# Output projection of a local-attention layer as three rounded products instead of one full float32 product

## Chip, cores and metric

One core of one Trainium2 chip. The metric is device time in microseconds (us) of one execution. "Rounded" stands for the type float32r of the program (printed as fp32r where it is written), "full float32" for plain f32.

## The reference

A sandwich of three blocks on x, 4 sequences of 512 tokens by 128 channels: x + 0.5 F(norm x), then a one-head attention whose softmax runs over an axis of length one, so that it is a sum of values, then x + 0.5 F(norm x) again. F has 6 layers of local attention and feed-forward. What the change touches is the last line of this:

```python
def attn_layer(x, Wqkv, qs, ksc, Wo):          # x: (4, 512, 128), 16 heads of 64
    q, k, v = split_heads(x @ Wqkv)
    q, k = l2norm(q) * qs, l2norm(k) * ksc      # then rotary embedding with scales
    out = local_attention(q, k, v)              # window 32, each looks one window back
    return merge_heads(out) @ Wo                # (4, 512, 1024) @ (1024, 128)
```

## The kernel before, in words

The work is cut in **units**: a unit is 128 tokens by 8 of the 16 heads (half h = U % 2). 8 units (UPS) make one sequence, 32 (UPL) one layer, 192 (UPP) one pass over the 6 layers; two passes make 384 units. All engines run the same loop over **slots** n (L1013 on TensorE, L607 ScalarE, L781 VectorE, L463 GpSimd, L356 the DMA queue of SyncE), and in a slot each takes its steps in an order written out by hand. Engines are kept in step by counting semaphores alone.

TensorE in slot n (L1014 to L1040): queries and keys of unit n+2 from Wqkv (project_qk), transposes of unit n (query_heads, key_heads), the mask, values of unit n (project_v), scores(n), in one slot of eight down (feed-forward), then transposes of the probabilities of unit n-1 (prob_major, L923), the output projection of unit n-2 (project_out, L951), and the weighing of values of unit n-1 (weigh_values, L934). In slots n%8 = 3, 4, 6 and 0 a step of the feed-forward follows; gated (n%8 = 0) is the long one.

project_out multiplies for each of 4 head pairs a 128x128 block of Wo (stationary) by ot (128x128, moving) and adds up in the PSUM tile tr0: 4 products in full float32. In the trace each is two LDWEIGHTS and two MATMUL of 128x128. The other projections are done with rounded numbers already: x and W are each split in a rounded high part and a rounded low part, and hi·hi + hi·lo + lo·hi is added up (project, L850; gated, L983). Each of these products is one LDWEIGHTS and one MATMUL.

ScalarE copies PSUM to SBUF: outputs(n-2) makes ot from o_ps (L573), weights_out(n-1) makes pt (L567), squares (L527), queries (L543), first_guess (L534, L537). VectorE: prob_sums(n-1) (L734, L737), rotate(n+2) (L699, L705), add_output(n-2) (L745), row_maxima and differences of n (L719, L726), square_sums(n+2) (L712). GpSimd: scale_probs(n-1) (L425), inverse_norms and normalise of n+1 (L433 to L448), then weight splitting where due, add_rotated(n+2) (L419).

Weights: Wqkv of the next layer comes in 6 blocks of 128x512 through a ring of two staging buffers: with m the slot in the layer, block m//4 is loaded at m%4 = 0 (load_block, L286), its high part is made by ScalarE at m%4 = 2 (split_high, L509), its low part by GpSimd at m%4 = 3 (split_low, L398). So splits fall in slots m = 3, 7, 11, 15, 19, 23. Wo comes in one DMA of 512 KB at m = 5 (load_wo, L296) to a double-buffered tile. At m = 11 GpSimd also splits W1 (L403), and at 13, 17, 21, 25 it makes rotary tables (L410).

Of the kernel before, what the change touches and what calls it, by code (L numbers as in the profile page):

```python
# [37 lines left out]
ONE, DMA_ONE = 1, 16  # L38
BLOCKS = 6
HS = SEQ // 2  # L40
# [35 lines left out]
def build(nc, x, w_qkv, w_o, Wqkv, Wo, W1, W2, scales_dram, vecs_dram, rot_dram, mask_dram, ident_dram, out):  # L76
    ctx = ExitStack()
    with ctx:
# [3 lines left out]
        def sem(name):  # L82
            return ctx.enter_context(nc.semaphore(name))
# [11 lines left out]
        staging = [sb(f"staging{i}", [P, HALF]) for i in range(2)]  # L95
        wqkv_hi = [sb(f"wqkv_hi{i}", [P, 3 * INNER], F32R) for i in range(2)]
        wqkv_lo = [sb(f"wqkv_lo{i}", [P, 3 * INNER], F32R) for i in range(2)]
        wo = [sb(f"wo{i}", [P, 2, PAIRS, P]) for i in range(2)]
        w1 = sb("w1", [P, 2 * HID])
# [35 lines left out]
        rden = [sb(f"rden{h}", [P, PAIRS * 2]) for h in range(2)]  # L135
        pt = [sb(f"pt{h}", [P, PAIRS, P]) for h in range(2)]
        ot = [sb(f"ot{h}", [P, 2, PAIRS, KEYS]) for h in range(2)]

# [141 lines left out]
        def _(sp):  # L280
# [5 lines left out]
            def load_block(g, b):  # L286

                k = g * BLOCKS + b
                if k >= 2:
                    sp.wait_ge(wqkv_split, k - 1)  # L290
                sp.dma_start(staging[k % 2][:, :], Wqkv[g % DEPTH, :, b * HALF:(b + 1) * HALF]).then_inc(block_in[k % 2], 16)

            def load_wo(g):

                sp.wait_ge(y_ready, ONE + UPL * max(0, g - 1))
                sp.dma_start(wo[g % 2][:, :, :, :].rearrange("p h a n -> p (h a n)"), Wo[g % DEPTH, :, :]).then_inc(wo_in, 16)  # L296

# [51 lines left out]
            for b in range(2, BLOCKS):  # L349
                load_block(0, b)  # L350
            load_wo(0)
            load_w1(0)
            load_w2(0)
            for p in range(PASSES):
                stage_tokens(p, p * SEQS * DEPTH)
                for n in slots(p):  # L356
                    if live(p, n):
                        shift_values(n)
                    if (it := staged_for(p, n, 0)) is not None:
                        stage_tokens(p, it)  # L360
                    if (it := ffn_of(p, n, MEAN_AT - 1)) is not None:
                        shift_ffn(it)
                    g, m = layer_slot(p, n)
                    if g + 1 < PASSES * DEPTH:
                        if m >= 0 and m % 4 == 0 and m // 4 < BLOCKS:
                            load_block(g + 1, m // 4)
                        if m == 5:
                            load_wo(g + 1)
                        if m == 13:
                            load_w1(g + 1)  # L370
                    if m == 12 and g > 0:
                        load_w2(g)
# [6 lines left out]
        def _(pool):  # L379
# [76 lines left out]
            for t in range(TPS):  # L456
                rotary_tables(0, t)
            for b in range(BLOCKS):
                split_low(0, b)
            for p in range(PASSES):  # L460
                for s in range(SEQS):
                    macaron_std(2 * p * SEQS + s)
                for n in slots(p):  # L463
                    if live(p, n - 1):
# [22 lines left out]
        def _(act):  # L487
# [16 lines left out]
            def split_high(g, b):  # L504

                k = g * BLOCKS + b
                act.wait_ge(block_in[k % 2], 16 * (k // 2 + 1))
                act.wait_ge(v_ready, ONE + UPL * max(0, g - 1))
                nc.scalar.activation(wqkv_hi[g % 2][:, b * HALF:(b + 1) * HALF], staging[k % 2][:, :], ACT.Copy  # L509
                                     ).then_inc(wqkv_hi_ready, 1)  # L510
# [53 lines left out]
            def weights_out(U):  # L564
                act.wait_ge(ptp_ready, ONE + U + 1)
                act.wait_ge(o_ready, ONE + max(0, U - 1))
                nc.scalar.activation(pt[U % 2][:, :, :].rearrange("p a n -> p (a n)"), tr1[:, :], ACT.Copy).then_inc(pt_ready, 1)  # L567

            def outputs(U):

                act.wait_ge(o_ready, ONE + U + 1)
                act.wait_ge(y_ready, ONE + max(0, U - 1))
                nc.scalar.activation(ot[U % 2][:, :, :, :].rearrange("p g a q -> p g (a q)"), o_ps[:, :, 0:PAIRS * KEYS],  # L573
                                     ACT.Copy).then_inc(ot_ready, 1)
# [22 lines left out]

            for b in range(BLOCKS):
                split_high(0, b)
            act.wait_ge(vecs_in, 32)  # L600
            nc.scalar.preload_act_table_set("natural_log_exp_and_others")
            for p in range(PASSES):
                for s in range(SEQS):
                    macaron_squares(2 * p * SEQS + s)
                act.wait_ge(zeros_ready, 8)
                tokens_high(p * SEQS * DEPTH)
                for n in slots(p):  # L607
                    after_gated = ffn_of(p, n - 1, GATED_AT) is not None
# [48 lines left out]
        def _(dve):  # L657
            for released in (summed, ss_ready, rot_parts, max_ready, dif_ready, rden_ready, y_added, xs_split,
                             fvar_ready, fn_ready, fn_split, hid_ready, xa_ready):
                dve.sem_inc(released, ONE)  # L660
# [69 lines left out]
            def prob_sums(U):  # L730
# [45 lines left out]
            for p in range(PASSES):  # L776
# [44 lines left out]
        def _(pe):  # L821
# [39 lines left out]
            def project_qk(U):  # L861
# [3 lines left out]
                if U % UPL == 0:  # L865
                    pe.wait_ge(wqkv_split, BLOCKS * (U // UPL + 1))
                project(qk_ps[:, 0, :], U, 0)
# [66 lines left out]
            def weigh_values(U):  # L934
# [3 lines left out]
                pe.wait_ge(vhead_in[h], TG * 16 + 16)  # L938
                pe.wait_ge(ot_ready, ONE + U)
                for a in range(PAIRS):  # L940
                    for ws in range(2):
                        for hp in range(2):
                            for gg in range(2):
# [3 lines left out]
                                    o_ps[hp * DH:(hp + 1) * DH, gg, at:at + WIN], (vn if ws else vs)[h][rows, 2 * a + hp, :],  # L947
                                    pt[h][rows, a, c * WIN:(c + 1) * WIN], start=True, stop=True, skip_group_check=True)
                last.then_inc(o_ready, 1)

            def project_out(p, U):  # L951
                h, g = U % 2, U // UPL
                pe.wait_ge(ot_ready, ONE + U + 1)
                if live(p, U + 2):
# [149 lines left out]
```

## Time and profile before

| | |
|---|---|
| time, median of 3 runs | 3490.75 us (3485.07 to 3491.98) |
| the profiled execution | 3489.94 us |
| its span, first to last instruction | 3488.1 us |
| mean granted TensorE clock | 0.983 |
| busy share PE, PEld, DVE, ACT, POOL | 95%, 77%, 75%, 63%, 75% |

PE is TensorE's matmul, PEld its weight load, which lies beside matmuls; DVE is VectorE, ACT ScalarE, POOL GpSimd, SP SyncE. A MATMUL record has the time until its last result, so neighbouring records overlap: what one costs in a row of them is the distance from start to start, and the busy share of PE says little. The chain of waits is followed back from the last instruction, each time to what released it; its times don't overlap.

### The profile page before, as it was taken

To read this page: it belongs to the slowest core of one execution; us is meant where nothing else is said; L and a number is where in the kernel's file an instruction comes from. 1 tells how busy PE (TensorE), PEld (TensorE's weight loads), DVE (VectorE), ACT (ScalarE), POOL (GpSimd) and SP (SyncE) were. 2 spreads that over 40 slices of the span, in tenths; PEclk is the share of its full clock that TensorE was granted. 3 is DMA by queue.
4 is the path that set the end of the run, shared out by engine and by line. 5 is a ranking of instruction groups with operands and counts; after the bars stand their busy time and mean duration, and the time that the engine had idled before them with its cause. 6 is when DMAs were issued, how large, how long until landed. Compare 5 with 4: busy or idle time off the path is not lost.

```text
span 3488.1 us, 149929 instructions
## 1 busy us (share of the span) xinstructions
PE 3326.3 (95%) x63806; PEld 2681.4 (77%) x63806; DVE 2632.2 (75%) x4403; ACT 2200.0 (63%) x4154; POOL 2606.3 (75%) x2894
## 2 busy tenths in 40 slices
PE   6999999999999999999789999999999999999997
PEld 4777778777777777877667777777777778778875
DVE  3777777877787877777458787778787778777773
ACT  3666666666666666666436666666666666666664
POOL 5877787787787777787348778877877877777772
PEclk8999999999999999999879999999999999999998
DMA  2222221221221222221112222212212212221111
GB/s 81 70 55 52 64 56 52 64 61 48 63 62 49 61 62 53 62 63 45 30 26 72 55 54 65 57 51 63 61 47 64 62 51 66 55 56 47 52 46 35
DMA packets 117856, 195.41 MB, mean 56 GB/s; under 512 B 23756, under 2 KB 36552, under 8 KB 117192
## 3 DMA queue, kind: packets, MB, share of 16 engines
q1 hardware_dynamic: 117192, 185.82, 19.6%
q8 instruction: 507, 8.31, 1.0%
q14 instruction: 157, 1.29, 0.1%
HBM read 33.71 MB, written 1.05 MB: 10 GB/s over the span
## 4 chain that ended last, share of the span: by engine, by line
PE 72%; POOL 16%; ACT 6%; issue 3%; DVE 1%; POOLq 0%; DMA 0%; ACTq 0%; SPq 0%; DVEq 0%
PE o_ps L946 10%; PE tr L961 8%; PE s_ps L917 7%; PE tr L930 5%; PE qk_ps L857 5%; POOL rotated L419 5%; PE qk_ps L859 4%; POOL rotated L448 4%; PE qk_ps L858 4%; PE f_ps L1007 4%; PE tr L884 4%; PE tr L857 3%; PE tr L897 3%; POOL prob L425 3%; ACT sq L527 2%
## 5 line engine op out<-in xcount | busy, mean ns | idle before, releaser
L419 POOL TENSOR_TENSOR rotated<-rotated 128x1024 f32<-128x1024 f32 x384 | 917.7, 2390 | 23.7 <-DVE rotated L705 23.7
L448 POOL TENSOR_TENSOR rotated<-rotated,rn 128x1024 f32<-128x1024 f32 x384 | 731.0, 1904 | 30.1
L425 POOL TENSOR_TENSOR prob<-prob,rden 128x512 f32<-128x512 f32 x384 | 436.6, 1137 | 417.2 <-DVE rden L737 413.4
L699 DVE TENSOR_TENSOR rotated<-qk_ps,rot 128x1024 f32<-128x1024 f32 x384 | 469.8, 1223 | 368.0 <-ACT sq L527 362.8
L705 DVE TENSOR_TENSOR rotated<-qk_ps,rot 128x512 f32<-128x512 f32 x768 | 490.4, 679 | 0.0
L917 PEld LDWEIGHTS s_ps<-kt,qt 64*32 64x32 f32 x24576 | 359.5, 107 | 139.6 <-issue 139.6
L712 DVE TENSOR_REDUCE ss_floor<-sq 128x16 f32<-128x1024 f32 x384 | 463.9, 1208 | 0.0
L573 ACT ACTIVATE ot<-o_ps 128x512 f32<-128x512 f32 x384 | 230.6, 601 | 317.4 <-PE o_ps L946 317.4
L917 PE MATMUL s_ps<-kt,qt 64*32 64x64 f32 x24576 | 421.5, 218 | 0.0
L543 ACT ACTIVATE qt<-tr 128x512 f32<-128x512 f32 x384 | 230.1, 599 | 294.5 <-PE tr L884 291.5
L961 PE MATMUL tr<-ot,wo 128*128 128x128 f32 x3072 | 414.6, 278 | 0.0
L527 ACT ACTIVATE sq<-qk_ps 128x1024 f32<-128x1024 f32 x384 | 397.5, 1035 | 17.6 <-PE qk_ps L859 17.6
L567 ACT ACTIVATE pt<-tr 128x512 f32<-128x512 f32 x384 | 229.7, 598 | 281.8 <-PE tr L930 281.7
L946 PE MATMUL o_ps<-pt,vs 64*64 64x32 f32 x12288 | 392.3, 222 | 1.4 <-ACT pt L567 1.4
L946 PE MATMUL o_ps<-pt,vn 64*64 64x32 f32 x12288 | 384.3, 219 | 0.0
L961 PEld LDWEIGHTS tr<-ot,wo 128*128 128x128 f32 x3072 | 374.1, 192 | 2.1 <-issue 1.2
L857 PE MATMUL qk_ps<-wqkv_hi,xs_hi 128*128 128x512 f32 x768 | 352.7, 459 | 21.2 <-DVE rotated L705 18.0
L946 PEld LDWEIGHTS o_ps<-pt,vs 64*64 64x64 f32 x12288 | 326.5, 134 | 48.1 <-ACT pt L567 1.9
L734 DVE TENSOR_REDUCE den<-prob 128x8 f32<-128x512 f32 x384 | 260.5, 678 | 126.0 <-ACT prob L553 125.7
L946 PEld LDWEIGHTS o_ps<-pt,vn 64*64 64x64 f32 x12288 | 328.7, 135 | 0.0
L859 PE MATMUL qk_ps<-wqkv_hi,xs_lo 128*128 128x512 f32 x768 | 306.5, 399 | 0.0
L858 PE MATMUL qk_ps<-wqkv_lo,xs_hi 128*128 128x512 f32 x768 | 305.0, 397 | 0.0
(151 smaller groups left out, 6960.5 us busy)
## 6 DMA issues: line engine op xcount, KB each, us to landing
vs<-vn SPq DMA_DIRECT2D x384, 192.0 KB
vs<-vtail SPq DMA_DIRECT2D x384, 64.0 KB, 2.5
vtail<-vn SPq DMA_DIRECT2D x384, 64.0 KB, 2.2
staging<-layer_wqkv_dram SPq DMA_DIRECT2D x72, 256.0 KB, 3.7
wo<-layer_wo_dram SPq DMA_DIRECT2D x12, 512.0 KB, 4.6
xs<-xa SPq DMA_DIRECT2D x48, 128.0 KB, 2.3
fs<-xa SPq DMA_DIRECT2D x48, 128.0 KB, 2.6
xs<-xa SPq DMA_DIRECT2D x48, 127.8 KB, 3.2
```

What stands on the lines that cost most here:

```text
L419: nc.gpsimd.tensor_tensor(rot_c[h], rot_c[h], rot_s[h], ALU.add).then_inc(rot_added, 1)
L425: nc.gpsimd.tensor_tensor(prob[h][:, :, :], prob[h][:, :, :], rden[h][:, :].unsqueeze(2).to_broadcast([P, 2 * PAIRS, KEYS]), ALU.mult).the ...
L448: nc.gpsimd.tensor_tensor(folded, folded, rn[:, :].unsqueeze(2).to_broadcast([P, 2 * UH, DH]), ALU.mult).then_inc(qkn_ready, 1)
L527: nc.scalar.activation(sq[:, :, :].rearrange("p a d -> p (a d)"), qk_ps[:, :, :].rearrange("p a n -> p (a n)"), ACT.Square, scale=SQUARE_S ...
L699: nc.vector.tensor_tensor(rot_c[h], src, part(0, 0, DH), ALU.mult)
L705: last = nc.vector.tensor_tensor(rot_s[h][:, :, :, to:to + H2], src[:, :, :, lo:lo + H2], part(1, lo, H2), ALU.mult)
L712: nc.vector.tensor_reduce(ss_floor[:, :, 0], sq[:, :, :], AX_X, ALU.add).then_inc(summed, 1)
L857: nc.tensor.matmul(dst, hi, wqkv_hi[g % 2][:, cols], start=True, stop=False)
L859: return nc.tensor.matmul(dst, lo, wqkv_hi[g % 2][:, cols], start=False, stop=True)
L917: last = nc.tensor.matmul(s_ps[c * WIN:(c + 1) * WIN, (2 * a + gg) * KEYS:(2 * a + gg + 1) * KEYS], qt[h][rows, a, w * WIN:(w + 1) * WIN], ...
L946: last = nc.tensor.matmul(o_ps[hp * DH:(hp + 1) * DH, gg, at:at + WIN], (vn if ws else vs)[h][rows, 2 * a + hp, :], pt[h][rows, a, c * WIN ...
L961: last = nc.tensor.matmul(tr0[:, 0:P], wo[g % 2][:, h, a, :], ot[h][:, :, a, :], start=a == 0, stop=a == PAIRS - 1)
```

## The change

Wo is no longer a tile of its own. It is loaded as blocks 6 and 7 of the staging ring and split into high and low parts that lie behind those of Wqkv. The attention outputs are split too: ScalarE's copy from o_ps is rounded (ot_hi), and a new VectorE instruction makes ot_lo = o_ps - ot_hi in slot n for unit n-2, after prob_sums(n-1). The o_ps tile is free again after that instruction. pt, ot_hi and ot_lo have one buffer each (pt and ot had two). project_out makes 12 rounded products in place of 4 full ones.

```diff
-BLOCKS = 6
+BLOCKS = 8
+WQKV_BLOCKS = 6
...
-        wo = [sb(f"wo{i}", [P, 2, PAIRS, P]) for i in range(2)]
...
+        pt = sb("pt", [P, PAIRS, P])
+        ot_hi = sb("ot_hi", [P, 2, PAIRS, KEYS], F32R)
+        ot_lo = sb("ot_lo", [P, 2, PAIRS, KEYS], F32R)
...
 load_block(g, b):
+                src = (Wqkv[g % DEPTH, :, b * HALF:(b + 1) * HALF] if b < WQKV_BLOCKS
+                       else Wo[g % DEPTH, :, (b - WQKV_BLOCKS) * HALF:(b - WQKV_BLOCKS + 1) * HALF])
+                sp.dma_start(staging[k % 2][:, :], src).then_inc(block_in[k % 2], 16)
...
-            load_wo(0)
...
-                        if m == 5:
-                            load_wo(g + 1)
...
 GpSimd and ScalarE at the start (split_low / split_high):
-            for b in range(BLOCKS):
+            for b in range(WQKV_BLOCKS):
...
+                if p == 0:          # after macaron_std / after tokens_high
+                    for b in range(WQKV_BLOCKS, BLOCKS):
+                        split_low(0, b)
...
 split_high:
-                act.wait_ge(v_ready, ONE + UPL * max(0, g - 1))
+                act.wait_ge(y_ready, ONE + UPL * max(0, g - 1))
...
 weights_out:
-                act.wait_ge(o_ready, ONE + max(0, U - 1))
+                act.wait_ge(o_ready, ONE + U)
...
 outputs:
-                act.wait_ge(y_ready, ONE + max(0, U - 1))
+                act.wait_ge(y_ready, ONE + U)
...
+            def outputs_low(U):
+                dve.wait_ge(ot_ready, ONE + U + 1)
+                nc.vector.tensor_tensor(ot_lo[:, :, :, :].rearrange("p g a q -> p g (a q)"), o_ps[:, :, 0:PAIRS * KEYS],
+                                        ot_hi[:, :, :, :].rearrange("p g a q -> p g (a q)").bitcast(F32), ALU.subtract
+                                        ).then_inc(ot_split, 1)
...
                     if live(p, n - 1):
                         prob_sums(n - 1)
+                    if live(p, n - 2):
+                        outputs_low(n - 2)
...
 project_qk:
-                    pe.wait_ge(wqkv_split, BLOCKS * (U // UPL + 1))
+                    pe.wait_ge(wqkv_split, BLOCKS * (U // UPL) + WQKV_BLOCKS)
...
 weigh_values:
-                pe.wait_ge(ot_ready, ONE + U)
+                pe.wait_ge(ot_split, ONE + U)
...
 project_out:
-                pe.wait_ge(ot_ready, ONE + U + 1)
+                pe.wait_ge(ot_split, ONE + U + 1)
...
-                    pe.wait_ge(wo_in, 16 * (g + 1))
+                    pe.wait_ge(wqkv_split, BLOCKS * (g + 1))
                 for a in range(PAIRS):
-                    last = nc.tensor.matmul(tr0[:, 0:P], wo[g % 2][:, h, a, :], ot[h][:, :, a, :],
-                                            start=a == 0, stop=a == PAIRS - 1)
+                    at = WQKV_BLOCKS * HALF + (h * PAIRS + a) * P
+                    hi, lo = wqkv_hi[g % 2][:, at:at + P], wqkv_lo[g % 2][:, at:at + P]
+                    nc.tensor.matmul(tr0[:, 0:P], hi, ot_hi[:, :, a, :], start=a == 0, stop=False)
+                    nc.tensor.matmul(tr0[:, 0:P], hi, ot_lo[:, :, a, :], start=False, stop=False)
+                    last = nc.tensor.matmul(tr0[:, 0:P], lo, ot_hi[:, :, a, :], start=False, stop=a == PAIRS - 1)
```

## Rows read from the trace of the kernel before

**Rows 1.** Page: chain of waits, share of the span by engine and line.
```profile
PE 72%; POOL 16%; ACT 6%; issue 3%; DVE 1%; POOLq 0%; DMA 0%; ACTq 0%; SPq 0%; DVEq 0%
PE o_ps L946 10%; PE tr L961 8%; PE s_ps L917 7%; PE tr L930 5%; PE qk_ps L857 5%; POOL rotated L419 5%; PE qk_ps L859 4%; POOL rotated L448 4%; PE qk_ps L858 4%; PE f_ps L1007 4%; PE tr L884 4%; PE tr L857 3%; PE tr L897 3%; POOL prob L425 3%; ACT sq L527 2%
```

**Rows 2.** Chain in order of time, 1513 to 1536 us: start, us, what.
```profile
1513.82 0.44 PE tr L884 x4
...
1516.94 0.58 PE tr L930 x4
1517.52 0.93 PE tr L961 x8
1518.45 1.06 PE o_ps L946 x64
...
1532.30 1.01 POOL prob L425
...
1533.35 0.65 PE tr L930 x4
1534.01 0.89 PE tr L961 x8
```

**Rows 3.** Waits: engine, tile, line, waited for: us in total, times, longest.
```profile
PEld tr L930 <- POOL prob L425: 68.7, 80, 3.9
DVE rotated L699 <- ACT sq L527: 362.8, 267, 4.2
```

**Rows 4.** Groups with shapes apart: busy us, mean ns of one, idle before.
```profile
L961 PEld LDWEIGHTS tr<-ot,wo 128*128 128x128 f32 x3072 | 374.1, 192 | 2.1 <-issue 1.2
L858 PEld LDWEIGHTS qk_ps<-wqkv_lo,xs_hi 128*128 128x128 f32 x768 | 146.2, 190 | 28.7 <-issue 11.0
L903 PEld LDWEIGHTS s_ps<-mask,ident 128*128 128x128 bf16 x384 | 37.6, 98 | 0.0
L973 PE MATMUL f_ps<-mean_mat,fsq 128*128 128x1 f32 x384 | 52.2, 257 | 2.3 <-ACT fd L580 2.3
```

**Rows 5.** Timeline, engine PE: start, us, then as above; L998 to L1000 are rounded.
```profile
1500.27 0.28 PE L998 MATMUL f_ps<-fn_hi,w_hi 128*128 128x256 f32 x1
...
1502.14 0.28 PE L999 MATMUL tr<-fn_lo,w_hi 128*85 128x256 f32 x1
...
1524.65 1.08 PE L961 MATMUL tr<-ot,wo 128*128 128x128 f32 x8
...
1535.89 1.05 PE L973 MATMUL f_ps<-mean_mat,fsq 128*128 128x1 f32 x8
```

**Rows 6.** Groups of DVE, POOL and ACT, columns as in rows 4.
```profile
L674 DVE TENSOR_TENSOR xa<-rotated,tr 128x512 f32<-128x512 f32 x6 | 4.1, 687 | 8.3 <-PE tr L846 8.3
L398 POOL TENSOR_TENSOR wqkv_lo<-staging,wqkv_hi 128x512 fp32r<-128x512 f32 x72 | 92.9, 1292 | 6.5 <-ACT wqkv_hi L509 6.5
L509 ACT ACTIVATE wqkv_hi<-staging 128x512 fp32r<-128x512 f32 x72 | 44.7, 622 | 8.7 <-DMA staging<-layer_wqkv_dram 8.7
```

**Rows 7.** Timeline of DVE, the slots n%8 = 2 and 3.
```profile
1515.47 0.74 DVE L774 SCALAR_TENSOR_TENSOR xa<-f_ps,vecs,xa 128x512 f32<-128x512 f32 x1
1516.33 1.22 DVE L699 TENSOR_TENSOR rotated<-qk_ps,rot 128x1024 f32<-128x1024 f32 x1
...
1522.24 0.20 DVE L737 RECIPROCAL rden<-den 128x8 f32<-128x8 f32 x1
1523.62 1.23 DVE L699 TENSOR_TENSOR rotated<-qk_ps,rot 128x1024 f32<-128x1024 f32 x1 [1.17 <-ACT sq L527]
```

**Rows 8.** Timeline of PE in slot n%8 = 0, with a split, then without.
```profile
1563.93 1.10 PE L917 MATMUL s_ps<-kt,qt 64*32 64x64 f32 x64
1565.74 0.66 PE L930 MATMUL tr<-ident,prob 128*128 128x128 f32 x4 [0.70 <-POOL prob L425]
...
320.34 1.10 PE L917 MATMUL s_ps<-kt,qt 64*32 64x64 f32 x64
321.37 0.66 PE L930 MATMUL tr<-ident,prob 128*128 128x128 f32 x4
```

More of the change, by code:

```diff
@@ L95, in build @@
         staging = [sb(f"staging{i}", [P, HALF]) for i in range(2)]
-        wqkv_hi = [sb(f"wqkv_hi{i}", [P, 3 * INNER], F32R) for i in range(2)]
-        wqkv_lo = [sb(f"wqkv_lo{i}", [P, 3 * INNER], F32R) for i in range(2)]
-        wo = [sb(f"wo{i}", [P, 2, PAIRS, P]) for i in range(2)]
+        wqkv_hi = [sb(f"wqkv_hi{i}", [P, BLOCKS * HALF], F32R) for i in range(2)]
+        wqkv_lo = [sb(f"wqkv_lo{i}", [P, BLOCKS * HALF], F32R) for i in range(2)]
         w1 = sb("w1", [P, 2 * HID])
@@ L135, in build @@
         rden = [sb(f"rden{h}", [P, PAIRS * 2]) for h in range(2)]
-        pt = [sb(f"pt{h}", [P, PAIRS, P]) for h in range(2)]
-        ot = [sb(f"ot{h}", [P, 2, PAIRS, KEYS]) for h in range(2)]
+        pt = sb("pt", [P, PAIRS, P])
+        ot_hi = sb("ot_hi", [P, 2, PAIRS, KEYS], F32R)
+        ot_lo = sb("ot_lo", [P, 2, PAIRS, KEYS], F32R)
         fs = sb("fs", [P, SEQ])
@@ L170, in build @@
         block_in = [sem(f"block_in{i}") for i in range(2)]
-        wo_in = sem("wo_in")
         w1_in = sem("w1_in")
@@ L213, in build @@
         ot_ready = sem("ot_ready")
+        ot_split = sem("ot_split")
         y_ready = sem("y_ready")
@@ L290, in load_block @@
                     sp.wait_ge(wqkv_split, k - 1)
[L291 to L296, printed above, removed]
+                src = (Wqkv[g % DEPTH, :, b * HALF:(b + 1) * HALF] if b < WQKV_BLOCKS
+                       else Wo[g % DEPTH, :, (b - WQKV_BLOCKS) * HALF:(b - WQKV_BLOCKS + 1) * HALF])
+                sp.dma_start(staging[k % 2][:, :], src).then_inc(block_in[k % 2], 16)
             def load_w1(g):
@@ L565, in weights_out @@
                 act.wait_ge(ptp_ready, ONE + U + 1)
-                act.wait_ge(o_ready, ONE + max(0, U - 1))
-                nc.scalar.activation(pt[U % 2][:, :, :].rearrange("p a n -> p (a n)"), tr1[:, :], ACT.Copy).then_inc(pt_ready, 1)
+                act.wait_ge(o_ready, ONE + U)
+                nc.scalar.activation(pt[:, :, :].rearrange("p a n -> p (a n)"), tr1[:, :], ACT.Copy).then_inc(pt_ready, 1)
             def outputs(U):
                 act.wait_ge(o_ready, ONE + U + 1)
-                act.wait_ge(y_ready, ONE + max(0, U - 1))
-                nc.scalar.activation(ot[U % 2][:, :, :, :].rearrange("p g a q -> p g (a q)"), o_ps[:, :, 0:PAIRS * KEYS],
+                act.wait_ge(y_ready, ONE + U)
+                nc.scalar.activation(ot_hi[:, :, :, :].rearrange("p g a q -> p g (a q)"), o_ps[:, :, 0:PAIRS * KEYS],
                                      ACT.Copy).then_inc(ot_ready, 1)
@@ L596, in gates @@
                                          bias=vecs[0:m, l, 3 + NCH + j:4 + NCH + j]).then_inc(gate_ready, 1)
-            for b in range(BLOCKS):
+            for b in range(WQKV_BLOCKS):
                 split_high(0, b)
@@ L606, in _ @@
                 tokens_high(p * SEQS * DEPTH)
+                if p == 0:
+                    for b in range(WQKV_BLOCKS, BLOCKS):
+                        split_high(0, b)
                 for n in slots(p):
@@ L657, in _ @@
         def _(dve):
-            for released in (summed, ss_ready, rot_parts, max_ready, dif_ready, rden_ready, y_added, xs_split,
+            for released in (ot_split, summed, ss_ready, rot_parts, max_ready, dif_ready, rden_ready, y_added, xs_split,
                              fvar_ready, fn_ready, fn_split, hid_ready, xa_ready):
@@ L947, in weigh_values @@
                                     o_ps[hp * DH:(hp + 1) * DH, gg, at:at + WIN], (vn if ws else vs)[h][rows, 2 * a + hp, :],
-                                    pt[h][rows, a, c * WIN:(c + 1) * WIN], start=True, stop=True, skip_group_check=True)
+                                    pt[rows, a, c * WIN:(c + 1) * WIN], start=True, stop=True, skip_group_check=True)
                 last.then_inc(o_ready, 1)
```

## The prediction, made before the changed kernel was run

> **What bounds the kernel now.** I read the chain of waits first, since busy shares mislead on TensorE. TensorE has 72% of the chain and GpSimd 16%; project_out (L961) alone has 8% of 3488 us, 279 us [rows 1]. So the step that the change rewrites lies on the path that sets the end. Next, the chain in order of time, to see how often it does: in slot n%8 = 2 it runs through prob_major, project_out and weigh_values without a gap, and eight L961 instructions hold it for 0.89 to 0.93 us. In the slot after, it leaves TensorE and comes back only by way of GpSimd's scale_probs (L425), at prob_major of the next slot, 1533.35. The project_out that TensorE did meanwhile isn't on the chain [rows 2]. The third view, the waits, counts these detours: TensorE waited 80 times for scale_probs, 68.7 us together, 0.86 us each [rows 3]. 384 - 80 = 304 units have their project_out on the chain; the share says 279 / 0.89 = 313. The two counts agree; I take 310.
>
> **The change part by part.**
>
> *project_out, instructions.* Before: 4 products, each two loads and two matmuls, 8 pairs. After: 3 rounded products for each of 4 pairs of heads, each one load and one matmul, 12 pairs. The question is what a rounded pair costs at 128 moving columns; no row has that. What sets the pace of the present pairs? L961 goes at 0.89 / 8 = 0.111 us a pair with 128 moving columns [rows 2]. L973, full float32 with the same 128x128 load but a single moving column, takes 1.05 us for 8 [rows 5], the last of them 0.257 us long [rows 4], so (1.05 - 0.257) / 7 = 0.113 us a pair. 128 columns or 1: the same pace, so it is the load that sets it. The rounded load is no shorter: 190 ns against 192 ns [rows 4]. Nearest rows for the rounded matmul are those of gated: from 1500.27 to 1502.14 there are 16 steps of 256 moving columns, 0.117 us each [rows 5]; the load fits into that. So a rounded pair at 128 columns should go at the pace of its load: **0.112 us**, between 0.110 (the transposes, four pairs of 128 columns in 0.44 us [rows 2], the quickest of that size) and 0.117 (the rounded row with 256 columns). 12 x 0.112 - 8 x 0.112 = **+0.448 us a unit**, between 12 x 0.110 - 0.896 = 0.42 and 12 x 0.117 - 0.896 = 0.51. The array has less to stream than before (12 x 128 columns once, against 4 products in full float32), but if it wasn't the streaming that set the pace, that buys nothing, and the loads went up by half.
>
> The Trainium skill (TensorE: Matmul & The Clock Gate, section LDWEIGHTS) gives a load the time of its columns at 1.2 GHz, 107 ns for 128, whatever the contraction; by that the sum would be 12 x 0.107 - 0.896 = 0.39 us a unit, an estimate, 120 us for 310 units. The trace agrees within 5 ns.
>
> *What of it reaches the end.* On 310 units in full: 310 x 0.448 = **139 us**. On the other 74 the growth eats TensorE's wait for scale_probs, which at 0.86 us on average is longer than 0.45, so it costs nothing there. If these detours were all shorter than that, it would be 384 units.
>
> *Does something hide the growth?* ScalarE's copy of pt lies beside project_out and is done before it already, since weigh_values, which needs both, follows project_out directly (1518.45 in rows 2); nothing is gained there.
>
> *The low part on DVE.* A new 128x512 tensor_tensor with one operand in PSUM and one in SBUF: 0.69 us as L674 [rows 6], 384 x 0.69 = 265 us of DVE. It stands after prob_sums, where DVE waits for squares in 267 of 384 slots, 362.8 us in all, 1.36 us each [rows 3]; there it is covered. The slot without cover is n%8 = 2: the feed-forward's L774 lies behind prob_sums too, and L699 starts at 1516.33 with no idle before it [rows 7]. There rotate(n+2) comes up to 0.69 us later, and with it add_output, row_maxima, differences and square_sums. The next prob_sums then ends about 0.7 us late (L737 at 1522.24 becomes 1522.9, ends 1523.1), the new low part ends at 1523.8, and L699 starts at 1523.62 plus the 0.45 us by which TensorE and so squares have moved: 1524.07. The delay is gone after one slot. GpSimd's scale_probs of that slot starts 0.7 us late, still before the guess of the norms that it waits for next. I take **0**; the bound is rival 3.
>
> *New waits.* project_out and weigh_values(n-1) wait for ot_split, counted up by outputs_low(n-2). Behind that wait stand the rest of TensorE's slot and all who wait for y and o. But before project_out TensorE has waited in prob_major(n-1) for scale_probs(n-1), which takes 1.01 us on the chain [rows 2] after the same prob_sums that outputs_low follows by 0.69: the low part is there first. In the slot of rows 7 it would be made by 1523.8 at the latest, and project_out starts at 1524.65 [rows 5], with the change later still. outputs_low's own wait for ot_ready is met: ScalarE makes outputs(n-2) ahead of the exponentials that prob_sums waits for. Price 0. One buffer of pt: weights_out(n-1) waits for weigh_values(n-2), which ran a slot before. One buffer of ot_hi: outputs(U) waits for project_out(U-1), which on TensorE stands just before the weigh_values(U) that it waits for anyway. split_high's wait on y_ready is met two slots before. All 0.
>
> *Wo through the ring.* Removed: 12 DMAs of 512 KB at m = 5. Added: 24 loads of 256 KB, at m = 24 and 28, on SyncE's queue in slots where the wait for the earlier split (m = 19, 23) is long met; they stand behind the shifts of values and ahead of nothing due in that slot. Added on ScalarE 24 x 0.622 = 15 us, in slots m = 26 and 30, beside waits; on GpSimd 24 x 1.29 = 31 us [rows 6], at m = 27 and 31, that is n%8 = 3 and 7 of the fourth sequence, the only one without splits so far. GpSimd's detour is what shows there: from the start of the scores to prob_major it is 1.81 us in slot n%8 = 0 behind a split and 1.03 us without one [rows 8], so today a split there costs 0.78 us. With TensorE 0.45 us longer per slot it costs 0.33: 11 x 0.33 = **+4 us**. The split at m = 27 is like the one of the third sequence, and costs nothing. At the start, blocks 6 and 7 are split by engines that wait for the first queries; a few tenths at most. Behind the last prefetched layer nothing is added.
>
> *Sum.* 139 + 4 = +143 us on the profiled execution, 3489.9 (its span 3488.1 and 1.8 around it): **3633 us**. The median of the runs is 0.8 us above it, which I let stand.
>
> **Rivals.**
>
> 1. *The rounded product has full price below 256 columns.* All rounded rows have 256 or 512 moving columns. If at 128 each product cost what the full one does, 2 x 0.112 us, a unit would take 12 x 0.224 = 2.69 us, +1.79; x 384 = 688, less the 69 us of waits that vanish: about **4110 us**. For it: no row excludes it. Against: one load and one matmul for each rounded product in every row. Chance 0.08.
>
> 2. *Faster: the rounded load is a quick one.* Its place is project_out, its price the pace of the matmul alone: half of the 0.117 us for 256 columns, 0.059; 12 x 0.059 = 0.70 us, 0.19 less than now; on 310 units -59, +9 for the Wo splits at their full 0.78 x 11: about **3440 us**. It decides from a pace under 0.896 / 12 = 0.075 us on. Against it: the bf16 load L903 takes 98 ns where the rounded one takes 190, which is the full one's time [rows 4]. The Trainium skill (TensorE: Matmul & The Clock Gate, section Weight-path perf modes) speaks for this rival: fast weight load is on for 128 weights of a type that isn't FP32, and a reader may count float32r there. The trace doesn't bear that out. Chance 0.05.
>
> 3. *DVE passes its 0.69 us on.* In 384 - 267 = 117 slots DVE had no wait for squares; if each handed on the whole 0.69, that is +81 us on top: **3714 us**. For it: DVE rises from 75% to about 80% of the span. Against: the slot worked out above. Chance 0.05.
>
> 4. *TensorE isn't held there after all,* the growth falls into waits that the chain doesn't show, and the time stays. Against: 310 units by two counts. Chance 0.01.
>
> **How the numbers follow.** Forecast 0.81: 3633. Its own bounds: 0.42 on 304 units, with 4, gives 3622; 0.51 on all 384, with 4, gives 3690. I widen below to 3590 for detours that absorb more than I count and above to 3715, which takes in the third rival. Left out are rivals 1, 2 and 4, 0.14 together. A measurement of this kernel tells about 0.2%, 7 us, from no change. Faster by more has the 0.05 of rival 2; within it the 0.01 of rival 4 and as much of the forecast's tail, 0.02; slower the rest, 0.93.
>
> **What would show it.** L961's place in the changed profile: 12 LDWEIGHTS and 12 MATMUL a unit, start to start 0.11 us; project_out about 1.34 us on the chain, its share up to 11 to 12%. TensorE's waits for scale_probs down from 68.7 us to 30 or 40, and GpSimd's share of the chain down slightly. DVE's idle before L699 down by most of 265 us less what the longer slots give back; outputs_low near 0.69 us with no idle before it. Wrong: a start to start of 0.06 or 0.21 us there, TensorE waiting for ot_split, or clock under 0.98.

## The result, and the profile after

The changed kernel takes 3615.98 us, median of 4 runs (3614.96 to 3620.19), against 3491.06 us for the kernel before: **1.0364 times as long** (95% interval 1.0346 to 1.0382), 125 us more. Forecast were 3633 us, +143. The profiled execution took 3615.14 us, its span is 3613.4 us.

Page of the changed kernel: busy time, then the chain by engine and by line, as [rows 1]. L955 is weigh_values (L946 before), L939 prob_major (L930), L972 to L974 the three products, L420 scale_probs (L425), L414 and L443 add_rotated and normalise.

```profile
PE 3480.6 (96%) x65342; PEld 2853.0 (79%) x65342; DVE 2871.6 (79%) x4787; ACT 2205.8 (61%) x4178; POOL 2618.0 (72%) x2918
PE 69%; POOL 17%; ACT 6%; issue 4%; DVE 3%; POOLq 0%; DMA 0%; ACTq 0%; DVEq 0%; SPq 0%
PE o_ps L955 9%; PE s_ps L926 6%; PE tr L939 5%; POOL rotated L414 5%; PE qk_ps L866 4%; POOL rotated L443 4%; PE tr L974 4%; PE tr L973 4%; PE f_ps L1019 4%; PE tr L972 3%; PE qk_ps L868 3%; PE qk_ps L867 3%; PE tr L893 3%; PE tr L866 3%; POOL prob L420 3%
...
L972 PE MATMUL tr<-ot_hi,wqkv_hi 128*128 128x128 f32 x1536 | 433.9, 282 | 0.4
L974 PE MATMUL tr<-ot_hi,wqkv_lo 128*128 128x128 f32 x1536 | 423.4, 276 | 0.0
L973 PE MATMUL tr<-ot_lo,wqkv_hi 128*128 128x128 f32 x1536 | 422.7, 275 | 0.0
```

project_out had 3072 MATMUL records and has 4608, one and a half times as many. Followed with one digit more, its three lines hold 10.9% of the chain, 394 us, against 8.2% and 286 us: +108 of the +125 us.

One unit, matmuls in order of time; first the kernel before, from prob_major to weigh_values:

```profile
1533.35 0.65 PE L930 MATMUL tr<-ident,prob 128*128 128x128 f32 x4 [0.84 <-POOL prob L425]
1533.84 1.06 PE L961 MATMUL tr<-ot,wo 128*128 128x128 f32 x8
1534.83 0.32 PE L946 MATMUL o_ps<-pt,vs 64*64 64x32 f32 x8
```

and the same stretch of the changed kernel:

```profile
1589.29 0.66 PE L939 MATMUL tr<-ident,prob 128*128 128x128 f32 x4 [0.47 <-POOL prob L420]
1589.69 0.31 PE L972 MATMUL tr<-ot_hi,wqkv_hi 128*128 128x128 f32 x1
1589.84 0.27 PE L973 MATMUL tr<-ot_lo,wqkv_hi 128*128 128x128 f32 x1
...
1590.39 0.28 PE L972 MATMUL tr<-ot_hi,wqkv_hi 128*128 128x128 f32 x1
...
1590.95 0.27 PE L974 MATMUL tr<-ot_hi,wqkv_lo 128*128 128x128 f32 x1
1591.16 0.32 PE L955 MATMUL o_ps<-pt,vs 64*64 64x32 f32 x8
```

From 1590.39 to 1590.95 five steps of 0.112 us: the pace that the forecast took. From the first product to weigh_values it is 1.47 us against 0.99, but the first product starts 0.40 us after the transposes begin where the full float32 one started after 0.49. So from prob_major to weigh_values this unit takes 1.87 us against 1.48: **+0.39 us, not +0.448**. Over 382 units of each trace the means say the same: 1.90 us against 1.50, +0.40. Of that, project_out itself is 0.455 us longer (1.465 against 1.010), as forecast, and the change-over before it is 0.05 us shorter (0.44 against 0.49).

The waits of the changed kernel, as [rows 3]:

```profile
DVE rotated L700 <- ACT sq L525: 209.6, 208, 4.9
...
PEld tr L939 <- POOL prob L420: 43.4, 77, 3.5
```

TensorE's waits for scale_probs fell from 68.7 to 43.4 us, VectorE's waits for squares from 362.8 to 209.6 us. And VectorE's share of the chain is 3%, not 1%. The place is the one that the forecast worked out, slot n%8 = 2. First the kernel before, with xs_lo, which lies ahead of the lines in [rows 7], and GpSimd's scale_probs beside it:

```profile
1514.91 0.64 DVE L684 TENSOR_TENSOR xs_lo<-xs,xs_hi 128x512 fp32r<-128x512 f32 x1
1515.08 1.38 POOL L425 TENSOR_TENSOR prob<-prob,rden 128x512 f32<-128x512 f32 x1 [1.08 <-DVE rden L737]
```

The changed kernel there, with the beginning of the next slot:

```profile
1569.58 0.68 DVE L735 TENSOR_REDUCE den<-prob 128x8 f32<-128x512 f32 x1
1570.29 0.20 DVE L738 RECIPROCAL rden<-den 128x8 f32<-128x8 f32 x1
1570.41 0.64 DVE L742 TENSOR_TENSOR ot_lo<-o_ps,ot_hi 128x512 fp32r<-128x512 f32 x1
1570.57 1.04 POOL L420 TENSOR_TENSOR prob<-prob,rden 128x512 f32<-128x512 f32 x1 [1.47 <-DVE rden L738]
1570.97 1.20 DVE L685 TENSOR_TENSOR xs_lo<-xs,xs_hi 128x512 fp32r<-128x512 f32 x1
1572.09 0.74 DVE L781 SCALAR_TENSOR_TENSOR xa<-f_ps,vecs,xa 128x512 f32<-128x512 f32 x1
1572.75 1.21 DVE L700 TENSOR_TENSOR rotated<-qk_ps,rot 128x1024 f32<-128x1024 f32 x1
...
1578.77 0.64 DVE L742 TENSOR_TENSOR ot_lo<-o_ps,ot_hi 128x512 fp32r<-128x512 f32 x1
1579.52 1.23 DVE L700 TENSOR_TENSOR rotated<-qk_ps,rot 128x1024 f32<-128x1024 f32 x1
```

No idle time in it: VectorE works without a break through slot 2, and in slot 3 too rotate (L700, at 1579.52) starts right behind the low part. In slot 3 VectorE waited for squares in all 48 cases before the change and waits in 8 of 48 after it; in slot 4 it waits in all 48 again. What was not expected is xs_lo, 1.20 us where it had been 0.64 us (the section on the hardware comes back to it).

### The profile page after: what moved, and what is told of

It reads as the page before. It is cut to its first block, busy times and chain, and to the rows that moved or that the text cites. A ratio compares the mean times of both kernels' runs of the same rounds, so it can differ in the third digit from the quotient of the medians.

```text
span 3613.4 us, 153470 instructions
## 1 busy us (share of the span) xinstructions
PE 3480.6 (96%) x65342; PEld 2853.0 (79%) x65342; DVE 2871.6 (79%) x4787; ACT 2205.8 (61%) x4178; POOL 2618.0 (72%) x2918
## 3 DMA queue, kind: packets, MB, share of 16 engines
HBM read 33.71 MB, written 1.05 MB: 10 GB/s over the span
## 4 chain that ended last, share of the span: by engine, by line
PE 69%; POOL 17%; ACT 6%; issue 4%; DVE 3%; POOLq 0%; DMA 0%; ACTq 0%; DVEq 0%; SPq 0%
PE o_ps L955 9%; PE s_ps L926 6%; PE tr L939 5%; POOL rotated L414 5%; PE qk_ps L866 4%; POOL rotated L443 4%; PE tr L974 4%; PE tr L973 4%; PE f_ps L1019 4%; PE tr L972 3%; PE qk_ps L868 3%; PE qk_ps L867 3%; PE tr L893 3%; PE tr L866 3%; POOL prob L420 3%
## 5 line engine op out<-in xcount | busy, mean ns | idle before, releaser
L414 POOL TENSOR_TENSOR rotated<-rotated 128x1024 f32<-128x1024 f32 x384 | 917.0, 2388 | 14.7 <-DVE rotated L706 14.7
L420 POOL TENSOR_TENSOR prob<-prob,rden 128x512 f32<-128x512 f32 x384 | 419.4, 1092 | 519.7 <-DVE rden L738 519.7
L443 POOL TENSOR_TENSOR rotated<-rotated,rn 128x1024 f32<-128x1024 f32 x384 | 731.5, 1905 | 30.3
L700 DVE TENSOR_TENSOR rotated<-qk_ps,rot 128x1024 f32<-128x1024 f32 x384 | 469.2, 1222 | 215.9 <-ACT sq L525 209.6
L571 ACT ACTIVATE ot_hi<-o_ps 128x512 fp32r<-128x512 f32 x384 | 230.5, 600 | 422.7 <-PE o_ps L955 422.0
L972 PE MATMUL tr<-ot_hi,wqkv_hi 128*128 128x128 f32 x1536 | 433.9, 282 | 0.4
L974 PE MATMUL tr<-ot_hi,wqkv_lo 128*128 128x128 f32 x1536 | 423.4, 276 | 0.0
L973 PE MATMUL tr<-ot_lo,wqkv_hi 128*128 128x128 f32 x1536 | 422.7, 275 | 0.0
L955 PE MATMUL o_ps<-pt,vs 64*64 64x32 f32 x12288 | 392.3, 222 | 1.4 <-ACT pt L565 1.4
L955 PE MATMUL o_ps<-pt,vn 64*64 64x32 f32 x12288 | 384.3, 219 | 0.0
L955 PEld LDWEIGHTS o_ps<-pt,vs 64*64 64x64 f32 x12288 | 326.5, 134 | 29.0 <-ACT pt L565 1.9
L955 PEld LDWEIGHTS o_ps<-pt,vn 64*64 64x64 f32 x12288 | 328.8, 135 | 0.0
```

Of the source, the lines that this page charges most:

```text
L414: nc.gpsimd.tensor_tensor(rot_c[h], rot_c[h], rot_s[h], ALU.add).then_inc(rot_added, 1)
L420: nc.gpsimd.tensor_tensor(prob[h][:, :, :], prob[h][:, :, :], rden[h][:, :].unsqueeze(2).to_broadcast([P, 2 * PAIRS, KEYS]), ALU.mult).the ...
L443: nc.gpsimd.tensor_tensor(folded, folded, rn[:, :].unsqueeze(2).to_broadcast([P, 2 * UH, DH]), ALU.mult).then_inc(qkn_ready, 1)
L700: nc.vector.tensor_tensor(rot_c[h], src, part(0, 0, DH), ALU.mult)
L955: last = nc.tensor.matmul(o_ps[hp * DH:(hp + 1) * DH, gg, at:at + WIN], (vn if ws else vs)[h][rows, 2 * a + hp, :], pt[rows, a, c * WIN:(c ...
L972: nc.tensor.matmul(tr0[:, 0:P], hi, ot_hi[:, :, a, :], start=a == 0, stop=False)
```

## The experiments

All ratios are to the kernel before, run on the same chip in the same session. Its median lay between 3487 and 3491 us from session to session, so a difference of times between two sessions is uncertain by about as much. The edits are shown cut: ... stands for lines left out, and arguments are shortened.

**What sets the pace of a product.** Two runs, each halving one side of the 12 products; where half the columns are loaded, the output is tr0[0:DH, 0:P]. Both leave half of each product out.

```diff
 e1_half_moving
-nc.tensor.matmul(tr0[:, 0:P], hi, ot_hi[:, :, a, :], ...)
+nc.tensor.matmul(tr0[:, 0:KEYS], hi, ot_hi[:, 0, a, :], ...)
 e2_half_load
-hi, lo = wqkv_hi[g % 2][:, at:at + P], wqkv_lo[g % 2][:, at:at + P]
+hi, lo = wqkv_hi[g % 2][:, at:at + DH], wqkv_lo[g % 2][:, at:at + DH]
...
```

> The 12 rounded products of project_out multiply 64 moving columns in place of 128 (half of the tokens of each unit get no output projection); the 12 loads of 128 columns stay. Theory (the load of the stationary block sets the pace of a pair): start to start stays 0.112 us, time 3616 us within 7. Rival (the streaming of the moving columns sets it, at a rounded price that is high for few columns): start to start halves to 0.056 us, project_out is 0.67 us shorter, time about 3430 us.

Measured: 3611.73 us, ratio 1.0359 (1.0343 to 1.0374). The fourth and the twelfth product of one unit of that run:

```profile
1580.36 0.28 PE L972 MATMUL tr<-ot_hi,wqkv_hi 128*128 128x64 f32 x1
...
1581.25 0.28 PE L974 MATMUL tr<-ot_hi,wqkv_lo 128*128 128x64 f32 x1
```

8 steps in 0.89 us, 0.111 us each. Half of the streaming gone, and neither the pace nor the time moves.

> The 12 products load 64 stationary columns in place of 128 (half of the output channels get no output projection); 128 moving columns stay. Theory (load sets the pace): start to start falls to about 0.06 us, where the 128 moving columns take over (half of the 0.117 us of 256 columns); project_out falls by 12 x 0.05 = 0.6 us, which on about 300 units is 180 us: 3435 us, with TensorE's waits for scale_probs back up to 70 us or more. Rival (a fixed price of 0.11 us for any LDWEIGHTS and MATMUL pair, whatever its columns): 3616 us, no change.

Measured: 3475.89 us, ratio 0.996 (0.9945 to 0.9975). The fourth and the twelfth product of one unit, and the chain by engine:

```profile
1582.38 0.22 PE L972 MATMUL tr<-ot_hi,wqkv_hi 128*64 128x128 f32 x1
...
1582.86 0.22 PE L974 MATMUL tr<-ot_hi,wqkv_lo 128*64 128x128 f32 x1
...
PE 49%; POOL 24%; DVE 12%; ACT 8%; issue 6%; POOLq 0%; DMA 0%; DVEq 0%; ACTq 0%; SPq 0%
```

8 steps in 0.48 us, 0.060 us each: the pace follows the loaded columns down, as the theory had it. A fixed price for each pair falls. Whether the 0.060 us is the shorter load (half of 0.112 is 0.056) or already the streaming of 128 columns (half of the 0.117 for 256 is 0.059), the run can't tell. The time missed its number, though: 3476 us, not 3435. TensorE's share of the chain fell from 69% to 49% and VectorE's rose to 12%, which reads as other engines holding the kernel from about 3500 us down. That asked for the next runs.

**More products.**

```diff
 e6_sixteen
+nc.tensor.matmul(tr0[:, 0:P], lo, ot_lo[:, :, a, :], start=False, stop=False)
```

> A fourth rounded product for each head pair, low times low: 16 loads in place of 12, everything else as in the changed kernel. Theory (a load of 0.112 us each, in full on the chain except where TensorE still waits for scale_probs, 77 times with some 0.35 us left): 384 x 0.448 = 172, less 77 x 0.35 = 27: 3761 us. Rival (TensorE waits for something else by now, which takes part of it): less than 3740 us.

Measured: 3763.32 us, ratio 1.0794 (1.0777 to 1.081), 2 us from the forecast. The chain by engine and the wait for scale_probs:

```profile
PE 92%; ACT 3%; issue 2%; DVE 1%; POOL 0%; DMA 0%; POOLq 0%; ACTq 0%; SPq 0%; DVEq 0%
...
PEld tr L939 <- POOL prob L420: 7.9, 6, 3.5
```

From 8 to 12 loads cost 125 us, from 12 to 16 cost 147 us (150 by the ratios). On the mean of its units the change-over is 0.44 us as with 12 loads, so the second step gets nothing back there, and the waits for scale_probs, 43.4 us with 12 loads, are down to 7.9 us in 6 waits.

**VectorE's low part.** One run takes it out of the changed kernel (TensorE waits for ot_ready in place of ot_split, and hi times ot_hi stands in for hi times ot_lo), one makes it twice (the second ahead of the first in outputs_low), one puts it into the kernel before, behind prob_sums(n - 1).

```diff
 e3_no_low
-                    if live(p, n - 2):
-                        outputs_low(n - 2)
...
 e5_two_lows
+nc.vector.tensor_tensor(ot_spare, o_ps, ot_hi, ALU.subtract)
 e9_before_low
+nc.vector.tensor_tensor(ot_lo, o_ps, ot[U % 2], ALU.subtract).then_inc(ot_split, 1)
```

> VectorE makes no low part (384 x 0.69 us less), project_out reads ot_hi in its place, TensorE waits for ot_ready in place of ot_split; the 12 products stay (hi times low is left out, hi times hi counted twice). Theory (the new instruction is covered by the wait for squares): 3616 us within 7, VectorE's wait for squares up again to 360 us or more. Rival (VectorE passes its 0.69 us on in the slots without cover): 20 to 80 us less, 3536 to 3596 us.

Measured: 3617.9 us, ratio 1.0373 (1.0357 to 1.0388), no change. VectorE's waits for squares are back up, at 387.2 us. At this length of TensorE's slot the low part costs nothing.

> VectorE makes the low part twice (the first one goes to a spare tile, as bf16): 384 x 0.69 us more of VectorE, everything else as in the changed kernel. Theory (the cover of one low part is all but used up in slots n%8 = 1 to 3, where the chain of the changed kernel already runs through VectorE, and holds in the others, where VectorE still waits for squares 0.56 us on the mean): the second one costs up to 0.69 us in two or three slots of each of 48 rounds of eight, 33 to 100 us: 3650 to 3715 us. Rival (VectorE is covered everywhere, a second low part costs nothing either): 3616 us. Rival (all of it comes out at the end): 265 us, 3880 us.

Measured: 3607.86 us, ratio 1.0337 (1.0322 to 1.0352). All three expectations missed: a second low part, 200 us more of VectorE, costs nothing and takes about 8 us off (the intervals just touch). TensorE's waits for scale_probs fell, from 43.4 us, to

```profile
PEld tr L942 <- POOL prob L421: 26.9, 48, 3.5
```

All of the fall lies in slot n%8 = 0: there from 25.6 us in 42 waits to 7.0 us in 2. Of the changed kernel, VectorE and GpSimd in that slot:

```profile
1620.15 0.64 DVE L742 TENSOR_TENSOR ot_lo<-o_ps,ot_hi 128x512 fp32r<-128x512 f32 x1
1620.70 0.82 DVE L766 SCALAR_TENSOR_TENSOR fn_lo<-fd,vecs,fn_hi 128x512 fp32r<-128x512 f32 x1
1620.93 1.49 POOL L420 TENSOR_TENSOR prob<-prob,rden 128x512 f32<-128x512 f32 x1
```

and with two low parts:

```profile
1618.74 0.68 DVE L745 TENSOR_TENSOR ot_lo<-o_ps,ot_hi 128x512 fp32r<-128x512 f32 x1
1618.95 1.05 POOL L421 TENSOR_TENSOR prob<-prob,rden 128x512 f32<-128x512 f32 x1
1619.33 1.22 DVE L769 SCALAR_TENSOR_TENSOR fn_lo<-fd,vecs,fn_hi 128x512 fp32r<-128x512 f32 x1
```

Where fn_lo is under way, scale_probs takes 1.49 us; where scale_probs started first it takes 1.05 us and fn_lo is the longer one, 1.22 us in place of 0.82. scale_probs is what TensorE waits for in that slot, fn_lo is not.

> The kernel before with VectorE's low part added and nothing else: ot stays full float32, project_out keeps its 8 loads, Wo stays as it is; the low part (o_ps - ot) is written to a tile that nobody reads, and o_ps is free again after it. Theory (VectorE's 0.69 us is covered only by the slots that project_out lengthened; the merged kernel, 46 us above before at the same number of loads, says so): 15 to 35 us above the kernel before, 3505 to 3525 us, with VectorE on the chain in slots n%8 = 1 to 3. Rival (the cover was there from the start, as the prediction had it): 3490 us.

Measured: 3502.2 us, ratio 1.0032 (1.002 to 1.0044): 11 us, a little under the bracket. The chain by engine:

```profile
PE 60%; POOL 16%; DVE 11%; ACT 6%; issue 6%; POOLq 0%; DMA 0%; DVEq 0%; ACTq 0%; SPq 0%
```

So the same instruction (0.64 us on the mean in both kernels, 0.69 was forecast) that is free in the changed kernel costs 11 us beside the short project_out.

**Fewer loads for the same products.** ot_hi and ot_lo behind each other, Wo's high part loaded once for both; add_output then adds two halves. A second run is the same without outputs_low, ot_hi in ot_lo's place.

```diff
 e4_merged
-nc.tensor.matmul(tr0[:, 0:P], hi, ot_hi[:, :, a, :], start=a == 0, stop=False)
-nc.tensor.matmul(tr0[:, 0:P], hi, ot_lo[:, :, a, :], start=False, stop=False)
+nc.tensor.matmul(tr0[:, 0:2 * P], hi, ot_both[:, :, :, a, :], start=a == 0, stop=a == PAIRS - 1, ...)
...
+nc.vector.tensor_tensor(cols, tr0[:, 0:P], cols, ALU.add).then_inc(y_half, 1)
+dve.wait_ge(y_half, U + 1)
+nc.vector.tensor_tensor(cols, tr0[:, P:2 * P], cols, ALU.add).then_inc(y_added, 1)
```

> The same three products with 8 loads in place of 12: ot_hi and ot_lo lie behind each other, Wo's high part is loaded once for both (256 moving columns, into two halves of tr0), then the low part with ot_hi (128 columns); VectorE adds the two halves of tr0 one after the other (a second add of 0.28 us). Theory (number of loads times 0.112 us): project_out is 4 x 0.117 + 4 x 0.112 = 0.92 us, 0.43 us less than with 12; about 310 x 0.40 = 124 us less, plus a few us for the second add: 3492 to 3515 us. Rival (the products' 12 x 128 columns set it, however they are cut): 3616 us or, with the second add, more.

Measured: 3536.69 us, ratio 1.0142 (1.0125 to 1.0159): 79 us less than the changed kernel, but 22 us above the bracket. 8 loads give most of the loss back, with all three products kept. The rest:

> The merged kernel (8 loads) without VectorE's low part: the high part is multiplied in its place (hi times low left out), the second add stays. Theory (what the merged kernel has above the kernel before is VectorE's): Wo's splits at their full 0.78 x 11 = 9 us and some of the second add: 3497 to 3508 us. Rival (the pairs of 256 and 128 columns in turn are slower than 0.112 us each, TensorE is the cause): 3537 us, as with the low part.

Measured: 3493.25 us, ratio 1.0005 (0.9996 to 1.0015), the time of the kernel before and a little below the bracket. So TensorE's part of the merged kernel is as cheap as the 8 full float32 loads (1.47 us from prob_major to weigh_values on the mean, 1.50 in the kernel before), and what lies between the two runs, 43 us (48 by the ratios), is the low part's. The chain by engine, with and without it:

```profile
PE 52%; POOL 20%; DVE 15%; issue 7%; ACT 6%; POOLq 0%; DMA 0%; DVEq 0%; ACTq 0%; SPq 0%
```

```profile
PE 64%; POOL 19%; ACT 7%; issue 5%; DVE 4%; POOLq 0%; DMA 0%; DVEq 0%; ACTq 0%; SPq 0%
```

Low part alone 11 us (on the kernel before); second add, Wo's splits and the slightly shorter stretch of TensorE about 2 together; all of it 48. The 2 us are a balance and not the price of the add: the table below has 8 us more in slot n%8 = 0, which follows a split, and up to 3 us less in the others. Add and low part together cost much more than either beside a short project_out.

**Wo through the ring.** Wo is split for the first layer alone: blocks 6 and 7 aren't loaded after it, and project_out reads wqkv_hi[0] and wqkv_lo[0].

```diff
 e8_wo_once
-k = g * BLOCKS + b
+k = g * WQKV_BLOCKS + b + (2 if g else 0)
...
```

> Wo is loaded and split for the first layer alone and used for all (the output projections of the other layers use the wrong Wo); the ring carries 6 blocks a layer after that. Theory (a split at m = 31 costs 0.33 us of GpSimd's detour, the one at m = 27 nothing): 3612 us, and in the trace the fourth sequence of a layer is about 0.4 us shorter from one slot n%8 = 0 to the next. Rival (the splits are covered): 3616 us and no difference there. Rival (ring and splits cost more than that, two splits of 1.3 us for each layer): 3585 us.

Measured: 3616.92 us, ratio 1.0359 (1.0344 to 1.0375). 4 us are too few for the times to tell. The trace tells them: ScalarE's copy of the first unit of the fourth sequence of the second layer, and that of the first unit of the next one; the changed kernel:

```profile
564.07 0.60 ACT L571 ACTIVATE ot_hi<-o_ps 128x512 fp32r<-128x512 f32 x1 [1.27 <-PE o_ps L955]
635.52 0.60 ACT L571 ACTIVATE ot_hi<-o_ps 128x512 fp32r<-128x512 f32 x1 [1.27 <-PE o_ps L955]
```

without the splits:

```profile
563.56 0.60 ACT L571 ACTIVATE ot_hi<-o_ps 128x512 fp32r<-128x512 f32 x1 [1.27 <-PE o_ps L955]
634.71 0.60 ACT L571 ACTIVATE ot_hi<-o_ps 128x512 fp32r<-128x512 f32 x1 [1.27 <-PE o_ps L955]
```

71.45 us against 71.15: 0.30 us, in each of 11 layers, 3.3 us; the spans differ by 3.4 us (3613.4 and 3610.0).

**Moving fn_lo.** If fn_lo lengthens scale_probs in slot 0, it should stand elsewhere. Both kernels, normed_low moved from behind prob_sums to behind rotate; in the merged one also xs_lo from slot n%8 = 2 to 5 (staged_for(p, n, 2) becomes staged_for(p, n, 5)).

```diff
-                    if (it := ffn_of(p, n, NORM_AT + 1)) is not None:
-                        normed_low(it)
                     if live(p, n + 2):
                         rotate(n + 2)
+                    if (it := ffn_of(p, n, NORM_AT + 1)) is not None:
+                        normed_low(it)
```

> The changed kernel with VectorE's fn_lo (normed_low, slot n%8 = 0) moved from behind prob_sums and the low part to behind rotate. Theory (the second low part of the earlier run made the kernel 8 us faster because it pushed fn_lo, whose operands all lie in SBUF, out of the time of GpSimd's scale_probs, 1.42 us in that slot and 1.04 in the others): scale_probs of slot n%8 = 0 falls to 1.04 us, TensorE waits for it there 0.3 us less, 48 x 0.3 = 14 us at most: 3602 to 3610 us. Rival (the 8 us are something else): scale_probs stays at 1.42 us or the time at 3616 us. Rival (fn_lo is now late for gated): above 3616 us.

Measured: 3630.91 us, ratio 1.0409 (1.0393 to 1.0424), 15 us above the changed kernel. GpSimd and VectorE in slot n%8 = 0, and the waits:

```profile
1625.98 1.04 POOL L420 TENSOR_TENSOR prob<-prob,rden 128x512 f32<-128x512 f32 x1
...
1628.22 1.90 POOL L443 TENSOR_TENSOR rotated<-rotated,rn 128x1024 f32<-128x1024 f32 x1
1628.97 1.69 DVE L766 SCALAR_TENSOR_TENSOR fn_lo<-fd,vecs,fn_hi 128x512 fp32r<-128x512 f32 x1
1630.08 2.84 POOL L414 TENSOR_TENSOR rotated<-rotated 128x1024 f32<-128x1024 f32 x1
...
PEld f_ps L1010 <- DVE fn_lo L766: 32.7, 46, 2.7
```

scale_probs has its 1.04 us, so the mechanism is right; and gated now waits for fn_lo, 46 times, which is the last of the rivals, and it costs more than was won. fn_lo isn't only late: at its new place it lies beside two other long GpSimd instructions, takes 1.69 us where it took 0.82, and lengthens the second of them from 2.38 to 2.84 us.

> The kernel before with the same move of fn_lo, nothing else. Theory as for the run above: scale_probs falls from 1.46 to 1.04 us in slot n%8 = 0, where three of four sequences wait 0.77 us for it: 36 x 0.4 = 14 us less: 3472 to 3480 us, faster than both kernels. Rival (rotate ends so late that fn_lo, 1.29 us, holds up gated, which follows in the same slot): 3491 to 3510 us.

Measured: 3517.11 us, ratio 1.0087 (1.0072 to 1.0102): slower by 30 us, 7 us above even the rival's bracket, with 52.6 us of waits for fn_lo. It takes 1.84 us on the mean there, not 1.29.

> The merged kernel (8 loads, two adds, with the low part) with xs_lo moved from slot n%8 = 2 to 5 and fn_lo behind rotate. Theory (its 44 us above the one without the low part are VectorE's in slots n%8 = 1 to 3, where xs_lo and the layer's residual add lie as well): 0.64 us less in 48 slots, 31 us, and up to 14 us for scale_probs in slot 0: 3492 to 3510 us. Rival (slots 1 to 3 are bound by the order of waits and not by VectorE's sum): 3520 to 3537 us.

Measured: 3527.22 us, ratio 1.0114 (1.0097 to 1.013): some 9 us less than merged, above the bracket and within the rival's. The run moved two things at once, and the late fn_lo holds up gated here too, 54.6 us in 46 waits. The time doesn't tell the two apart; the trace does, slot by slot.

**The same runs by slot.** A step is the time from one start of weigh_values to the next, and belongs to the slot of the second; gated of slot n%8 = 0 follows weigh_values and so lies in the step of slot 1. The steps of all units summed by slot, us:

| | n%8 = 0 | 1 | 3 | the others |
|---|---|---|---|---|
| kernel before | 373.6 | 636.7 | 349.8 | 1900.6 |
| with the low part (e9) | 373.0 | 637.0 | 364.0 | 1900.7 |
| with late fn_lo (e12) | 359.6 | 682.4 | 349.6 | 1899.8 |
| merged, no low part (e10) | 381.9 | 635.6 | 348.7 | 1897.8 |
| merged (e4) | 381.5 | 636.9 | 392.5 | 1898.2 |
| merged, both moved (e11) | 362.5 | 687.9 | 348.7 | 1897.6 |
| changed kernel | 382.6 | 655.0 | 369.1 | 1982.1 |
| two low parts (e5) | 369.8 | 655.4 | 370.2 | 1983.8 |
| changed, late fn_lo (e13) | 369.5 | 680.9 | 369.1 | 1986.4 |

The low part's price, 14 us on the kernel before and 44 in the merged one, lies in slot n%8 = 3 alone, the one behind the slot where VectorE has xs_lo and the residual add as well. The merged kernel with both moves has none of the 44 left, and moving fn_lo changes nothing in slot 3 in the other two kernels: so that is what xs_lo's move is worth. The late fn_lo takes 13 to 19 us off in slot 0, where scale_probs is quick again, and puts 26 to 51 us on the step that has gated. The second low part of the changed kernel wins the same 13 us and doesn't hold up gated. By these sums the merged kernel with xs_lo moved alone would come out at about 3537 - 44 = 3493 us, an estimate; it wasn't run. No version that keeps the whole computation and was run beats the kernel before.

## Why the prediction was right, and where its terms were off

*The load sets the pace, 8 loads become 12.* Right. 0.112 us was taken and 0.112 us measured, halving the moving columns changed nothing (e1), halving the loaded ones nearly halved it (e2), 16 loads came out 2 us from what the pace says (e6). Rivals 1 and 2, the full price and the quick load, are both off the table; the rounded load takes 192 ns, as the full one did.

*+0.448 us a unit.* Mis-sized by 0.05: measured +0.40 on the mean. The term that was off is "12 x 0.112 - 8 x 0.112": it priced the pairs, rightly (project_out is 0.455 us longer), and took the change-over from the transposes as unchanged. A rounded first product starts 0.44 us after the transposes begin, the full one after 0.49. 310 x 0.40 = 124 us, and with the 3 us of Wo it is 127, against 125 measured. The forecast's sum was 18 us too high, nearly all of it this term. That the forecast's other estimate, 0.39 us, lies closer to the growth measured is luck: the loads went at 0.112 us each, and the time was saved ahead of them.

*310 of 384 units.* Right, and more exactly than its working deserved. Laid side by side, 310 of the 382 steps that both traces have are longer by over 0.25 us, by 0.4 as a rule, and the other 72 hardly at all. The two counts behind it, 304 and 313, were rounded: with 8.2% for 8% the second is 320. The wait for scale_probs fell by 25 us; the forecast named 30 or 40 as what would be left, and 43 are.

*VectorE's low part at nothing.* Right for the changed kernel (e3), but the reasons given hold only in part. The forecast had one slot without cover and the delay gone in the next. In the trace before, VectorE had no wait for squares in 31 of 48 slots n%8 = 0, 44 of 48 slots 1 and 42 of 48 slots 2, and after the change the delay, made longer by xs_lo's 0.56 us, is gone only in slot 4. TensorE doesn't feel it: slots 2 and 3 are as long with the low part as without. Part of this cover came out of TensorE's own growth: with project_out short again, the same instruction costs 11 us (e9) or, with a second add, 43 (e4 against e10). Asking slot by slot what the cover is made of would have found this in the forecast: the 362.8 us of waits for squares don't lie in the slots that need them.

*Wo at +4 us.* Right: 3.3 us in the trace.

*Not seen at all:* the quicker scale_probs. In slot 2 it fell from 1.37 to 1.04 us on the mean, since the low part, which reads PSUM, now lies beside it and xs_lo comes later. It is worth nothing here: TensorE waited for scale_probs in slots 0, 4 and 6 alone, before the change as after it.

## What to carry to other kernels

At 128 stationary and 128 moving columns a rounded product costs a load, and so does each of the two halves of a full float32 one: three rounded products lose to one full product by 12 loads to 8. Count loads first, and where one stationary block serves two moving ones, put these behind each other and load it once; here this gave back 79 of 125 us. And a cover is a property of a slot, not of an engine's idle total: an instruction that is free beside a long step can cost when that step is cut.

## What the runs showed of the hardware

**VectorE and GpSimd hold each other up, and who starts first keeps its time.** scale_probs of 1.04 us takes 1.49 when fn_lo is under way, and fn_lo takes 1.22 when scale_probs started first (the rows of the second low part). fn_lo's own time is 0.70 us, in the kernel before, where it started first; in the changed kernel's 0.82 the end of a GpSimd instruction lies at its start:

```profile
872.19 0.70 DVE L759 SCALAR_TENSOR_TENSOR fn_lo<-fd,vecs,fn_hi 128x512 fp32r<-128x512 f32 x1
872.35 1.44 POOL L425 TENSOR_TENSOR prob<-prob,rden 128x512 f32<-128x512 f32 x1 [0.35 <-DVE rden L737]
...
1618.60 2.38 POOL L414 TENSOR_TENSOR rotated<-rotated 128x1024 f32<-128x1024 f32 x1
```

xs_lo, 0.64 us before the change, where it started first and scale_probs took 1.38, takes 1.20 us in the changed kernel, where scale_probs is under way. VectorE instructions with one operand in PSUM (the low part, rotate) do nothing of the kind: scale_probs is 1.04 to 1.05 us beside them. The Trainium skill (SBUF — State Buffer, section SBUF: two separate sides) says this: the two engines share a pair of ports, which a GpSimd instruction or a VectorE one with two SBUF inputs takes for its whole length while the other waits. The traces agree in who is held up. The delays of these cases are 0.34 to 0.56 us, each 0.08 to 0.15 us less than what the first instruction had left.

**A rounded product after the transposes starts sooner** than a full float32 one, 0.44 against 0.49 us on the mean of 382 units in either trace (0.40 and 0.49 in the rows above). Why was not tried.
